# 64x64 products in the inverse of the first layer, and scores of the second layer from two-part splits with two heads in the halves of TensorE's rows

## The chip, the cores and the metric

One core of a Trainium2 chip runs the whole program. The metric is the device time of one execution in microseconds (us), as the median of several executions of the same kernel. TensorE multiplies (PE in the profile, its weight loads PEld), VectorE is DVE, ScalarE is ACT, GpSimd is POOL, and SyncE (SP) issues most DMAs.

## What is computed

Eight batches of 512 tokens with 256 features pass four stages, each added to its input: an attention layer with landmarks, a feed-forward layer with experts, a causal attention layer with rotary embedding, and the feed-forward layer again. The change touches the first and the third.

```python
# first layer: 16 heads, for each (batch, head) a 64x64 matrix attn2
z = swapaxes(a, -1, -2) / (max(col) * max(row))
for _ in range(6):
    az = a @ z
    z = 0.25 * z @ (13 * I - az @ (15 * I - az @ (7 * I - az)))
out = attn1 @ z @ (attn3 @ v)
# second attention layer: 16 heads of 16 features, T = 512
scores = einsum('bhqd,bhkd->bhqk', rotary(q), rotary(k)) * 16 ** -0.5
attn = softmax(where(causal, -inf, scores))
out = einsum('bhqk,bhkd->bhqd', attn, v) @ Wo.T
```

## The kernel before

Each layer is a block in which every engine has its own program, written in the order in which it runs; PSUM banks are handed over by semaphores (class `Fills`: a consumer waits for `full`, TensorE waits for `free`). TensorE's order is the order of the code.

**First layer (`layer_a`).** It runs batch by batch, about 110 us each. The heads stand in eight pairs, one head in partitions 0 to 63 and one in 64 to 127. The inverse of a batch is a chain of steps (`INVERSE_STEPS`), and each step is placed by `mark` between products of other work, so that VectorE and ScalarE have time to answer. Most products of the chain (line 960) are made of two 64x64 ones, in opposite quarters of the array. In the step "wz" TensorE multiplies with `p_diag`, the block-diagonal form of the polynomial: in four of the six iterations one 128x128 product per pair gives both W and Z (line 992). In the third iteration (`RESTORE`, k = 2) each pair takes two 64x64 products (line 988) and then one with all 128x128 weights and 64 columns (line 990), and in the last iteration the latter alone. A product of plain fp32 is two instructions in the trace.

**Second attention layer (`layer_b`).** The 16 heads of a batch are 8 pairs, 64 pairs in all. Queries and keys are projected (line 2644), rotated by VectorE and POOL, and split into three bf16 parts whose sum is the fp32 number (`high` and `middle` on ScalarE, `split_rest` on POOL). The parts go through DRAM (`spread` on SP) into `stacked`: six groups of 16 rows, so that one product over 96 rows sums the six products of parts that matter. Four such buffers are in use.

The program goes in slots, one per pair. In slot n the turned scores (keys in the rows, kind "st") of pair n and the plain scores (kind "s") of pair n + 7 are made, so that the row maxima are known seven slots before they are needed: VectorE takes them from the plain scores (`maximum`, lines 2379 and 2383), POOL splits them into three parts, TensorE turns them (line 2653), and they come back through DRAM as three more rows of the turned product (99 rows). ScalarE takes the exponentials of the turned scores (line 2506).

The causal scores of a pair are five units of 512 columns, `UNITS`: two of one product (line 2606 writes the mask, line 2616 the scores), two of two products (384 and 128 columns, mask by line 2610), and one with both heads in it (256 columns each, line 2602). The mask is a bf16 product of an identity with a triangle, and the scores are added to it in the bank. In each slot TensorE takes, for u = 0 to 4, unit u turned and then unit u plain; behind u = 1 the early side work (`misc_early`: transposes of x, projections, turning of the maxima), behind u = 2 the products with v (`products`, line 2674, in 128x32 tiles), behind u = 3 the late side work (`misc_late`: transposes and output projection). "st" has three banks, "s" two, the products with v one and the side work two.

## Time and profile before

| | us |
|---|---|
| median of 3 runs | 2464.02 |
| lowest, highest | 2453.02, 2469.33 |
| the profiled execution, its whole time | 2465.51 |
| span of its trace, first to last instruction | 2463.4 |
| TensorE busy in the span | 2220.4 |
| mean granted TensorE clock | 0.945 of full speed |

The first layer runs from the start to 1000 us with its landmarks, the second attention layer from about 1470 to 2015, and the feed-forward layers between and behind. Durations of products in the trace hold their way through the array, and products overlap: how fast they go is read from the distance of their starts.

### The profile page before, as it was taken

The numbers are of one execution on the slowest core, as the hardware profiler recorded it, in microseconds if no ns is written. First come the engines' busy times: TensorE is split into PE (matmuls) and PEld (weight loads), VectorE is DVE, ScalarE is ACT, GpSimd is POOL, SyncE is SP. The second block draws the span as 40 slices with busy tenths as digits, with TensorE's granted clock in tenths as the row PEclk, the third lists the DMA queues.
The fourth block names the chain that finished last, engine by engine and source line by source line (L and its number), as shares of the span: only waits on it lengthen the run. The fifth ranks groups of instructions, "written<-read, shape, count | busy, mean of one in ns | idle before, by whom it ended". The sixth has DMA issues, their size and how long they took to land. (4 is left out here: it accounts for less than half of the span.)

```text
span 2463.4 us, 49191 instructions
## 1 busy us (share of the span) xinstructions
PE 2220.4 (90%) x19494; PEld 1810.1 (73%) x19494; DVE 1457.2 (59%) x3308; ACT 1030.9 (42%) x1986; POOL 680.1 (28%) x772
## 2 busy tenths in 40 slices
PE   7799999999999999699879974899999979986998
PEld 7688888888888888577669972455555547776998
DVE  2565564647465554388746644666666627874665
ACT  4333334333333334244335531455555544432554
POOL 3210110101010100165522222433343215652222
PEclk8899999999999999799989986899999999998999
DMA  7300000000000000411547756444444416113775
GB/s 233 117 18 10 10 10 10 10 10 19 2 18 10 10 1 2 130 44 61 206 157 220 235 147 140 79 79 79 80 86 80 74 55 223 48 43 95 233 231 137
DMA packets 155901, 212.68 MB, mean 86 GB/s; under 512 B 51656, under 2 KB 140000, under 8 KB 150368
## 3 DMA queue, kind: packets, MB, share of 16 engines
q1 hardware_dynamic: 142140, 191.38, 27.6%
q0 software_dynamic: 12864, 17.38, 4.3%
q8 instruction: 158, 2.59, 0.4%
q10 hardware_dynamic: 672, 0.79, 0.2%
q14 instruction: 67, 0.55, 0.1%
HBM read 141.80 MB, written 67.69 MB: 85 GB/s over the span
## 5 line engine op out<-in xcount | busy, mean ns | idle before, releaser
L2383 DVE TENSOR_REDUCE b_neg_max<-bank 128x1 f32<-128x512 f32 (+2 forms) x384 | 179.0, 507 | 140.4 <-PE bank L2616 137.9
L2506 ACT ACTIVATE b_probsT<-bank 128x512 f32<-128x512 f32 x320 | 183.1, 603 | 180.2 <-PE bank L2616 155.0
L2113 PE MATMUL bank<-e_hT_hi,k_rwkv 128*128 128x256 f32 x1088 | 214.8, 283 | 2.8 <-DVE e_hT_lo L2016 2.8
L2113 PEld LDWEIGHTS bank<-e_hT_hi,k_rwkv 128*128 128x128 f32 x1088 | 177.0, 191 | 3.6 <-DVE e_hT_lo L2016 3.6
L789 POOL TENSOR_TENSOR probs<-probs,rcp 128x512 f32<-128x512 f32 x64 | 66.9, 1045 | 381.7 <-DVE rcp L658 381.7
L2127 PE MATMUL bank<-v_rwkv_hi,e_hidden_hi 128*128 (+1 forms) x544 | 153.5, 282 | 0.0
L2127 PE MATMUL bank<-v_rwkv_hi,e_hidden_lo 128*128 (+1 forms) x544 | 153.5, 282 | 0.0
L2113 PE MATMUL bank<-e_hT_lo,k_rwkv 128*128 128x256 f32 x544 | 152.3, 280 | 0.0
L2127 PE MATMUL bank<-v_rwkv_lo,e_hidden_hi 128*128 (+1 forms) x544 | 152.1, 280 | 0.0
L2074 ACT ACTIVATE e_relu<-bank,k_bias 128x256 f32<-128x256 f32 x272 | 113.6, 469 | 73.2 <-PE bank L2113 63.1
L2616 PE MATMUL bank<-b_k_stacked,b_q_stacked 96*128 96x512 bf16 (+3 forms) x512 | 126.5, 309 | 0.0
L2616 PE MATMUL bank<-b_q_stacked,b_k_stacked 99*128 99x512 bf16 (+3 forms) x512 | 121.7, 300 | 0.0
L960 PEld LDWEIGHTS bank<-pi_t,wz 64*64 64x64 f32 x3072 | 97.2, 134 | 32.7 <-issue 23.1
L960 PE MATMUL bank<-pi_t,wz 64*64 64x64 f32 x3072 | 110.4, 221 | 3.5 <-DVE pi_t L700 3.5
L640 DVE TENSOR_TENSOR conv_lo<-bank,conv_hi 128x512 fp32r<-128x512 f32 x64 | 44.3, 692 | 109.8 <-ACT conv_hi L805 109.8
L2035 DVE TENSOR_TENSOR e_square<-e_relu 128x512 f32<-128x512 f32 x136 | 93.9, 690 | 23.9 <-ACT e_relu L2074 16.7
L2113 PEld LDWEIGHTS bank<-e_hT_lo,k_rwkv 128*128 128x128 f32 x544 | 103.8, 191 | 0.0
L2037 DVE TENSOR_TENSOR e_hidden_lo<-e_square,e_hidden_hi 128x512 fp32r<-128x512 f32 x136 | 94.2, 692 | 14.8 <-DVE e_square L2035 0.5
L2606 PE MATMUL bank<-masks,ident 128*128 128x128 bf16 x256 | 57.5, 225 | 50.2 <-DMA b_k_stacked<-scratch_b_parts 34.2
L2127 PEld LDWEIGHTS bank<-v_rwkv_hi,e_hidden_lo 128*128 128x128 f32 x544 | 102.4, 188 | 0.0
L2127 PEld LDWEIGHTS bank<-v_rwkv_lo,e_hidden_hi 128*128 128x128 f32 x544 | 102.4, 188 | 0.0
L2127 PEld LDWEIGHTS bank<-v_rwkv_hi,e_hidden_hi 128*128 128x128 f32 x544 | 102.2, 188 | 0.0
(364 smaller groups left out, 6252.4 us busy)
## 6 DMA issues: line engine op xcount, KB each, us to landing
k_rwkv<-scratch_k SPq DMA_DIRECT2D x32, 2048.0 KB, 7.3
scratch_b_parts<-b_part SPq DMA_DIRECT2D x96, 128.0 KB, 2.1
b_q_stacked<-scratch_b_parts SPq DMA_DIRECT2D x96, 128.0 KB, 4.4
b_k_stacked<-scratch_b_parts SPq DMA_DIRECT2D x96, 128.0 KB, 4.6
e_rows<-scratch_rows SPq DMA_DIRECT2D x34, 258.0 KB, 7.7
scratch_rows<-f_hq SPq DMA_DIRECT2D x16, 516.0 KB, 8.1
x_tokens<-in_x_dram SPq DMA_DIRECT2D x8, 512.0 KB, 8.0
scratch_x_out<-x_tokens SPq DMA_DIRECT2D x8, 512.0 KB, 2.9
```

The source lines that it names most:

```text
L640: nc.vector.tensor_tensor(lo, fills.data(*name)[:], hi.bitcast(F32), ALU.subtract).then_inc(fills.released(*name), 1)
L789: nc.gpsimd.tensor_tensor(probs, probs, spread(rcp1[:, f], NP), ALU.mult).then_inc(s["probs1_done"], 1)
L960: last = nc.tensor.matmul(data[h, j * M:(j + 1) * M], lhs[h, j], rhs[h, j], start=True, stop=True)
L2035: nc.vector.tensor_tensor(flat(sq[:, q % 2]), flat(r[:, q % 2]), flat(r[:, q % 2]), ALU.mult).then_inc(s["square_done"], 1)
L2037: nc.vector.tensor_tensor(flat(h2[1][:, q % SQ_RING]), flat(sq[:, q % 2]), flat(h2[0][:, q % SQ_RING]).bitcast(F32), ALU.subtract).then_in ...
L2074: nc.scalar.activation(r[:, q % 2, n], fl.data("h", q)[:, n * ROWS:(n + 1) * ROWS], ACT.Relu, bias=ff.k_bias[i % 2][:, 2 * c + n:2 * c + n ...
L2113: last = nc.tensor.matmul(data[:, half * ROWS:(half + 1) * ROWS], ff.k_part(i % 2, a)[:, k, at:at + P], hT[b][:, i % 2, k], start=n == 0, ...
L2127: last = nc.tensor.matmul(fl.data("e", i)[:, t * C:(t + 1) * C], h2[a][:, q % SQ_RING, half, t * P:(t + 1) * P], values[b], start=chunk == ...
L2383: last = nc.vector.tensor_reduce(neg_max[:, half % 2, t, head + e:head + e + 1], data[:, at:at + (t + 1) * P], AX_X, ALU.max, negate=True)
L2506: nc.scalar.activation(probsT[:, ring, u], fl.data("st", pair, u)[:], ACT.Exp, scale=DB ** -0.5).then_inc(fl.released("st", pair, u), 1)
L2606: nc.tensor.matmul(data[:, at:at + P], ident16[:], mask[:, 0:P], start=True, stop=False, skip_group_check=True)
L2616: last = nc.tensor.matmul(data[:, at:at + size], weights[:, tile:tile + P], moving[:, first:first + size], start=False, stop=True, skip_gr ...
```

## The change

In the inverse the product of line 990 is made of two 64x64 ones, one for each head of the pair, as line 988 is. Line 992 stays as it is.

In the second attention layer:

- Queries, keys and maxima are split into two fp32r parts instead of three bf16 ones. ScalarE's `middle` and one subtraction on POOL are gone (and on VectorE for the first keys); the split of the maxima takes two steps instead of five. Three groups of 16 rows, and two of maxima, are 48 or 50 rows, and two heads stand in rows 0 to 63 and 64 to 127.
- A score product uses 64 rows of the array. In slots that have both kinds, `scores_beside` issues a product of the turned unit and one of the plain unit by turns, always with the heads in opposite halves and in two banks. Units are taken in the order 0, 1, both heads, 2, 3 (turned) and 2, 3, both heads, 0, 1 (plain).
- The mask takes two products per unit and head, since an identity of 64 rows covers half of the mask's rows.
- In the unit of both heads the halves would write one bank, so TensorE waits (`wait_for_heads`) for the first head's products to end before it issues the second's. It stands behind u = 1 and its side work instead of last.
- The maxima are turned by fp32 products. The stores are two per step instead of three, the loads still twelve per half of a batch, in rows of 2 KB instead of 1 KB; loads of maxima are two instead of one.

```diff
                                         nc.tensor.matmul(pairs[h, j, 0], wz[h, g, j, 1, :], p_diag[h, g, j, h], start=True, stop=True)
                                 if k in (RESTORE, ITERS - 1):
-                                    last = nc.tensor.matmul(pairs[:, j, 1], p_diag[:, g, j], wz[:, g, j, 1, :], start=True, stop=True)
+                                    for h in halves:
+                                        last = nc.tensor.matmul(pairs[h, j, 1], p_diag[h, g, j, h], wz[h, g, j, 1, :], start=True, stop=True)
                                 else:
                                     last = nc.tensor.matmul(pairs[:, j], p_diag[:, g, j], wz[:, g, j], start=True, stop=True)
...
-Q_PARTS, K_PARTS_B = (0, 0, 1, 1, 0, 2), (0, 1, 0, 1, 2, 0)
+Q_PARTS, K_PARTS_B = (0, 0, 1), (0, 1, 0)
+PARTS_B = 2
 STACK = len(Q_PARTS) * DB
-MAX_PARTS = 3
+MAX_PARTS = 2
+ROW_HALF = P // 2
+STACK_DMAS = 2 * 2 * len(Q_PARTS)
...
+BOTH = len(UNITS) - 1
+TURNED_ORDER, SCORED_ORDER = (0, 1, BOTH, 2, 3), (2, 3, BOTH, 0, 1)
...
-        ident16, masks = buf("ident16", [P, P], BF16), buf("masks16", [P, 2, 2 * P], BF16)
+        ident16, masks = buf("ident16", [P, 2, P], BF16), buf("masks16", [P, 2, 2, P], BF16)
...
-        parts = [buf(f"b_part{c}", [P, 2, T], BF16) for c in range(3)]
-        stacked = [[buf(f"b_{side}_stacked{b}", [P, HEADS_H, T], BF16) for b in range(STACK_BUFS)] for side in ("q", "k")]
-        neg_max, rest = buf("b_neg_max", [P, 2, TT, HEADS_H]), buf("b_max_rest", [P, TT, HEADS_H])
-        max_parts, max_rows = buf("b_max_parts", [P, 2, TT, MAX_PARTS, HEADS_H], BF16), buf("b_max_rows", [P, 2, T], BF16)
-        one_rows = buf("b_one_rows", [P, T], BF16)
+        parts = [buf(f"b_part{c}", [P, 2, T], F32R) for c in range(PARTS_B)]
+        stacked = [[buf(f"b_{side}_stacked{b}", [P, PAIRS_H, T], F32R) for b in range(STACK_BUFS)] for side in ("q", "k")]
+        neg_max = buf("b_neg_max", [P, 2, TT, HEADS_H])
+        max_parts, max_rows = buf("b_max_parts", [P, 2, TT, MAX_PARTS, HEADS_H], F32R), buf("b_max_rows", [P, 2, T])
         v = buf("b_v", [P, 2, TT, HB, 2 * DB])
         probsT = buf("b_probsT", [P, PROBS_RING, len(UNITS), T])
-        oT = buf("b_oT", [P, T])
+        one_rows = oT = buf("b_oT", [P, T])
...
-        scratch = lambda name, shape: nc.dram_tensor(f"scratch_{name}", shape, BF16, kind="Internal").ap()
-        parts_out, max_out = scratch("b_parts", (B * 4, 3, P, T)), scratch("b_max", (B * 2 + 1, MAX_PARTS * HEADS_H, T))
+        scratch = lambda name, shape: nc.dram_tensor(f"scratch_{name}", shape, F32, kind="Internal").ap()
+        parts_out, max_out = scratch("b_parts", (B * 4, PARTS_B, P, T)), scratch("b_max", (B * 2 + 1, MAX_PARTS * HEADS_H, T))
...
+                def stack(side, b, at):
+                    for row, c in enumerate((Q_PARTS, K_PARTS_B)[side]):
+                        for e in range(2):
+                            first = e * ROW_HALF + row * DB
+                            sp.dma_start(stacked[side][b][first:first + DB, :, :].bitcast(F32),
+                                         parts_out[at, c].rearrange("(j e d) t -> e d j t", e=2, d=DB)[e]).then_inc(stack_loaded[b], 16)
...
-                    g.tensor_tensor(rotated[:, at % 2], rotated[:, at % 2], parts[0][:, at % 2], ALU.subtract).then_inc(s["rest_done"], 1)
-                    ready((s["mid_done"], at + 1))
-                    g.tensor_tensor(parts[2][:, at % 2], rotated[:, at % 2], parts[1][:, at % 2], ALU.subtract).then_inc(s["lo_done"], 1)
+                    g.tensor_tensor(parts[1][:, at % 2], rotated[:, at % 2], parts[0][:, at % 2].bitcast(F32), ALU.subtract).then_inc(
+                        s["lo_done"], 1)
...
-                            exponentials(slot, u)
+                            exponentials(slot, TURNED_ORDER[u])
...
+                def mask(data, pair, u, turned, e, roll, start):
+                    rows = half_rows(e)
+                    region, src = data[:].rearrange("p (n k) -> p n k", k=P), masks[rows, int(turned), roll, :]
+                    if u == BOTH:
+                        region = region[:, 2 * e + (0 if turned else 1), :]
+                    elif len(UNITS[u]) == 1:
+                        region = region[:, 0 if turned else 3, :]
+                    else:
+                        region = region[:, 0:2, :] if turned else region[:, 0:4:3, :]
+                        src = src.unsqueeze(1).to_broadcast([ROW_HALF, 2, P])
+                    nc.tensor.matmul(region, ident16[rows, roll, :], src, start=start, stop=False, skip_group_check=True)
+                def part(data, pair, u, turned, e, n):
+                    b, j = half_of(pair) % STACK_BUFS, pair % PAIRS_H
+                    rows = half_rows(e, STACK + MAX_PARTS if turned else STACK)
+                    q, k = stacked[0][b][rows, j], stacked[1][b][rows, j]
+                    t, at = UNITS[u][e if u == BOTH else n][1:]
+                    size = (t + 1) * P
+                    tile, first = ((TT - 1 - t) * P, (TT - 1 - t) * P) if turned else (t * P, 0)
+                    weights, moving = (k, q) if turned else (q, k)
+                    return nc.tensor.matmul(data[:, at:at + size], weights[:, tile:tile + P], moving[:, first:first + size], start=False,
+                                            stop=True, skip_group_check=True)
+                def alone(one, start):
+                    for roll in range(2):
+                        mask(*one, roll, start and roll == 0)
+                    for n in range(parts_in(one[2])):
+                        last = part(*one, n)
+                    return last
+                def beside(one, other, start):
+                    for roll in range(2):
+                        mask(*one, roll, start and roll == 0)
+                        mask(*other, roll, start and roll == 0)
+                    for n in range(parts_in(one[2])):
+                        last = part(*one, n), part(*other, n)
+                    return last
+                heads_done = 0
+                def wait_for_heads(*last):
+                    nonlocal heads_done
+                    for instruction in last:
+                        instruction.then_inc(s["head_done"], 1)
+                        heads_done += 1
+                    pe.wait_ge(s["head_done"], heads_done)
                 def scores(pair, u, turned):
                     name = ("st" if turned else "s", pair, u)
-                    b, head = half_of(pair) % STACK_BUFS, pair % PAIRS_H * 2
-                    rows = slice(0, STACK + MAX_PARTS) if turned else slice(0, STACK)
-                    data = begin(*name)
-                    mask = masks[:, int(turned)]
-                    if u == last_unit:
-                        at = 0 if turned else P
-                        region = data[:].rearrange("p (h n) -> p h n", h=2)[:, :, at:at + P]
-                        nc.tensor.matmul(region, ident16[:], mask.rearrange("p (h n) -> p h n", h=2), start=True, stop=False,
-                                         skip_group_check=True)
-                    elif len(UNITS[u]) == 1:
-                        at = 0 if turned else 3 * P
-                        nc.tensor.matmul(data[:, at:at + P], ident16[:], mask[:, 0:P], start=True, stop=False, skip_group_check=True)
+                    one = (begin(*name), pair, u, turned)
+                    if u == BOTH:
+                        wait_for_heads(alone((*one, 0), True))
+                        last = alone((*one, 1), False)
                     else:
-                        region = data[:, 0:2 * P] if turned else data[:].rearrange("p (h n) -> p h n", h=4)[:, 0:4:3, :]
-                        src = mask if turned else mask.rearrange("p (h n) -> p h n", h=2)
-                        nc.tensor.matmul(region, ident16[:], src, start=True, stop=False, skip_group_check=True)
-                    for e, t, at in UNITS[u]:
-                        size = (t + 1) * P
-                        q, k = stacked[0][b][rows, head + e], stacked[1][b][rows, head + e]
-                        tile, first = ((TT - 1 - t) * P, (TT - 1 - t) * P) if turned else (t * P, 0)
-                        weights, moving = (k, q) if turned else (q, k)
-                        last = nc.tensor.matmul(data[:, at:at + size], weights[:, tile:tile + P], moving[:, first:first + size], start=False,
-                                                stop=True, skip_group_check=True)
+                        last = alone((*one, UNITS[u][0][0]), True)
                     last.then_inc(fl.filled(*name), 1)
+                def scores_beside(pair, u, ahead, w):
+                    one, other = (begin("st", pair, u), pair, u, True), (begin("s", ahead, w), ahead, w, False)
+                    if u == BOTH:
+                        wait_for_heads(*beside((*one, 0), (*other, 1), True))
+                        last = beside((*one, 1), (*other, 0), False)
+                    else:
+                        last = beside((*one, UNITS[u][0][0]), (*other, UNITS[w][0][0]), True)
+                    last[0].then_inc(fl.filled("st", pair, u), 1)
+                    last[1].then_inc(fl.filled("s", ahead, w), 1)
...
-                                                    max_parts[:, (n * 2 + name[2]) % 2, t].rearrange("p c h -> p (c h)"), ident16[:], start=True,
-                                                    stop=True)
+                            last = nc.tensor.matmul(data[ROWS, t * P:(t + 1) * P],
+                                                    max_parts[:, (n * 2 + name[2]) % 2, t].rearrange("p c h -> p (c h)").bitcast(F32),
+                                                    core.ident[:], start=True, stop=True)
...
+                        if turned_at(slot) is not None and pair is not None:
+                            scores_beside(slot, TURNED_ORDER[u], pair, SCORED_ORDER[u])
+                        elif pair is not None:
+                            scores(pair, SCORED_ORDER[u], False)
+                        elif turned_at(slot) is not None:
+                            scores(slot, TURNED_ORDER[u], True)
```

TensorE's order, in the third iteration of the inverse (the `wz` step of one group of pairs). Before:

```order
L988 MATMUL bank<-pi_p_diag,wz 64x64 x2
L990 MATMUL bank<-wz,pi_p_diag 128x64
L988 MATMUL bank<-pi_p_diag,wz 64x64 x2
L990 MATMUL bank<-wz,pi_p_diag 128x64
L988 MATMUL bank<-pi_p_diag,wz 64x64 x2
L990 MATMUL bank<-wz,pi_p_diag 128x64
```

The same place on TensorE now:

```order
L988 MATMUL bank<-pi_p_diag,wz 64x64 x2
L991 MATMUL bank<-wz,pi_p_diag 64x64 x2
L988 MATMUL bank<-pi_p_diag,wz 64x64 x2
L991 MATMUL bank<-wz,pi_p_diag 64x64 x2
L988 MATMUL bank<-pi_p_diag,wz 64x64 x2
L991 MATMUL bank<-wz,pi_p_diag 64x64 x2
```

Every product with 128x64 shape has become two of 64x64, and nothing else has moved there.

TensorE's order in one slot of the second attention layer, from a unit of two parts on (`masks` is the mask product, `b_q_stacked` as the moving side the turned scores, `b_k_stacked` the plain ones). Before:

```order
L2610 MATMUL bank<-masks,ident 128x2x128
L2616 MATMUL bank<-b_k_stacked,b_q_stacked 128x384
L2616 MATMUL bank<-b_k_stacked,b_q_stacked 128x128
L2602 MATMUL bank<-masks,ident 128x2x128
L2616 MATMUL bank<-b_q_stacked,b_k_stacked 128x256 x2
L2602 MATMUL bank<-masks,ident 128x2x128
L2616 MATMUL bank<-b_k_stacked,b_q_stacked 128x256 x2
L2606 MATMUL bank<-masks,ident 128x128
L2616 MATMUL bank<-b_q_stacked,b_k_stacked 128x512
L2606 MATMUL bank<-masks,ident 128x128
L2616 MATMUL bank<-b_k_stacked,b_q_stacked 128x512
```

The same place on TensorE now, from a unit of two parts to the next unit:

```order
L2608 MATMUL bank<-masks,ident 128x256
L2608 MATMUL bank<-masks,ident 128x2x128
L2608 MATMUL bank<-masks,ident 128x256
L2608 MATMUL bank<-masks,ident 128x2x128
L2618 MATMUL bank<-b_q_stacked,b_k_stacked 128x384
L2618 MATMUL bank<-b_k_stacked,b_q_stacked 128x384
L2618 MATMUL bank<-b_q_stacked,b_k_stacked 128x128
L2618 MATMUL bank<-b_k_stacked,b_q_stacked 128x128
L2608 MATMUL bank<-masks,ident 128x128 x4
L2618 MATMUL bank<-b_q_stacked,b_k_stacked 128x512
L2618 MATMUL bank<-b_k_stacked,b_q_stacked 128x512
```

The turned and the plain unit are no longer one behind the other but alternate product by product, with two mask products for each, and the unit of both heads has left this place.

## Rows read from the trace of the kernel before

**Rows 1.** The page, busy time of each engine over the span (us, share, instructions):

```profile
PE 2220.4 (90%) x19494; PEld 1810.1 (73%) x19494; DVE 1457.2 (59%) x3308; ACT 1030.9 (42%) x1986; POOL 680.1 (28%) x772
```

**Rows 2.** Windows of 20 us: us, busy PE, PEld, DVE, ACT, POOL, granted clock, DMA:

```profile
256.00:276.00 20.00, 20.00 (x180) 15.65 (x180) 11.56 (x23) 7.35 (x18) 3.13 (x3) 0.83 0.08 27
...
921.00:941.00 20.00, 20.00 (x228) 15.84 (x227) 13.38 (x28) 8.68 (x20) 4.25 (x5) 1.00 0.01 2
```

**Rows 3.** Timeline of TensorE in the third iteration: start, us, line, operation, count:

```profile
369.24 0.39 PE L904 MATMUL bank<-u_lo,a_xnT_hi 128*128 128x512 f32 x1
369.47 0.39 PE L904 MATMUL bank<-u_hi,a_xnT_lo 128*128 128x512 f32 x1
369.84 0.33 PE L988 MATMUL bank<-pi_p_diag,wz 64*64 64x64 f32 x4
370.10 0.43 PE L990 MATMUL bank<-wz,pi_p_diag 128*128 128x64 f32 x2
370.47 0.33 PE L988 MATMUL bank<-pi_p_diag,wz 64*64 64x64 f32 x4
...
378.68 0.63 PE L927 MATMUL bank<-a_xnT_hi,g_lo 128*128 128x512 f32 x1
```

**Rows 4.** Timeline of TensorE, other steps of the first layer:

```profile
334.64 1.95 PE L1023 MATMUL bank<-kl_diag,wqT 128*128 128x128 f32 x16
336.52 1.15 PE L960 MATMUL bank<-pi_t,wz 64*64 64x64 f32 x32
...
415.69 2.00 PE L990 MATMUL bank<-wz,pi_p_diag 128*128 128x64 f32 x16
```

**Rows 5.** Windows of the second layer, columns as in rows 2:

```profile
1600.00:1656.00 56.00, 51.09 (x401) 29.42 (x400) 35.33 (x82) 29.94 (x58) 21.43 (x23) 1.00 0.52 87
...
1936.00:2006.00 70.00, 65.47 (x576) 38.25 (x575) 29.37 (x64) 44.37 (x85) 5.52 (x13) 1.00 0.20 34
```

**Rows 6.** Timeline of TensorE in one slot of the second layer:

```profile
1702.24 0.27 PE L2602 MATMUL bank<-masks,ident 128*128 128x256 bf16 x1
...
1702.91 0.22 PE L2606 MATMUL bank<-masks,ident 128*128 128x128 bf16 x1
1702.96 0.38 PE L2616 MATMUL bank<-b_q_stacked,b_k_stacked 99*128 99x512 bf16 x1
1703.18 0.22 PE L2606 MATMUL bank<-masks,ident 128*128 128x128 bf16 x1
...
1703.46 0.27 PE L2610 MATMUL bank<-masks,ident 128*128 128x256 bf16 x1
...
1703.97 0.38 PE L2616 MATMUL bank<-b_k_stacked,b_q_stacked 96*128 96x384 bf16 x2
...
1707.06 0.38 PE L2616 MATMUL bank<-b_k_stacked,b_q_stacked 96*128 96x512 bf16 x1
1707.37 0.86 PE L2674 MATMUL bank<-b_probsT,b_v 128*32 128x256 f32 x16
```

**Rows 7.** Timeline of VectorE, the maxima of three units:

```profile
1526.93 1.35 DVE L2383 TENSOR_REDUCE b_neg_max<-bank 128x1 f32<-128x512 f32 x3 [2.84 <-PE bank L2616]
1528.22 0.69 DVE L2379 TENSOR_REDUCE b_neg_max<-bank 128x2 f32<-128x512 f32 x1
```

**Rows 8.** Lines 2616 and 1084: durations ns min/median/max, first and last start us:

```profile
L2616 PEld LDWEIGHTS bank<-b_q_stacked,b_k_stacked x512: 97/98/151, 1557.4 to 2005.2; 99*128 99x128 bf16 x171
L2616 PE MATMUL bank<-b_q_stacked,b_k_stacked x512: 217/320/634, 1557.5 to 2005.4; 99*128 99x512 bf16 x44, 99*128 99x256 bf16 x43, 99*128 99x384 bf16 x42, 99*128 99x128 bf16 x42
...
L1084 PEld LDWEIGHTS bank<-g_hi,conv_lo x256: 187/188/193, 202.7 to 995.3; 128*128 128x128 f32 x128
```

**Rows 9.** Line 2653 as in rows 8, and POOL's timeline of the first split:

```profile
L2653 PE MATMUL bank<-ident,b_max_parts x64: 219/219/314, 1548.9 to 1980.9; 128*24 128x128 bf16 x64
...
1493.60 1.15 POOL L2458 TENSOR_TENSOR b_part<-b_rotated,b_part 128x512 bf16<-128x512 f32 x1 [0.74 <-ACT b_part L2521]
```

**Rows 10.** Waits of TensorE, 1513 to 2006 us: total, times, longest:

```profile
PE bank L2606 <- DMA b_k_stacked<-scratch_b_parts: 34.2, 9, 23.3
```

110 lines of the change are left out of this document (49 added, 61 removed).

## Prediction

> **What bounds the kernel now.** I read the page first, for the shares of the engines and TensorE's clock, then tables of windows for the two places that the diff touches, then TensorE's timeline inside them, then the waits. The page says that TensorE is busy for 90% of the span [rows 1], so the question in each place is whether TensorE is what the stage waits for.
>
> In the first layer it is: in 20 us around one step of the inverse TensorE is busy for all 20, while VectorE is idle for 7 to 8 of them [rows 2]. The step meant is the third iteration's (k = 2, RESTORE), where line 988 (64x64) and line 990 (128x128 weights) alternate. The timeline shows three things. Ordinary products of 512 columns start every 0.23 us at the high clock (369.24, 369.47) [rows 3]. The alternating step has one round, four short and two long instructions, in 0.63 us (369.84 to 370.47) [rows 3], and it holds eight rounds in each of the eight batches. And the clock falls in it: at 378.68 a product of the same kind takes 0.63 us instead of 0.39 [rows 3], and the window has a mean granted clock of 0.83 against 1.00 in a batch where it does not fall [rows 2]. Of eight such windows three have 0.83, two 0.91 and three 1.00. So this is a step in which TensorE mostly empties and refills, long enough to bring its own clock down from 2.4 to 1.2 GHz.
>
> In the second layer TensorE is busy for 51.1 of 56 us, VectorE for 35.3 [rows 5]. The timeline of one slot [rows 6] gives the price of each pair of score units (turned and not): unit of two heads 0.67 us (1702.24 to 1702.91), unit of one part 0.55 (to 1703.46), unit of two parts 0.66 by its columns. Five of them, 2 x 0.55 + 2 x 0.66 + 0.67, are 3.1 us per slot. VectorE's maxima need nearly as much: three reductions of 1.35 us in a row for a one-part and a two-part unit, and 0.69 for a unit of two heads [rows 7], so about 0.61 and 0.68 per unit at pace, 3.2 us per slot. A slot takes 7.0 us (64 of them from 1557.5 to 2005.4) [rows 8]. Scores have only two banks, so TensorE can be two units ahead of VectorE and no more.
>
> **The inverse.** (a) In RESTORE the two long instructions of a round become four 64x64 ones. 64x64 products run at 32 in 1.15 us, of which the last one's own 0.22 is its way through the array: 0.030 us each [rows 4]. A round of eight is 0.24 us, 0.39 less; 64 rounds: 24.7 us. (b) In the last iteration 16 long instructions take 2.00 us [rows 4], 0.115 each, 1.84 in all; 32 short ones 0.96. Eight times 0.88 is 7 us. (c) The step becomes 1.9 us instead of 5, and no longer holds a stretch of emptying long enough for the clock to fall, as far as these rows tell. The fall cost (1 - clock) x 20 us per window: 3 x 3.4 + 2 x 1.8 = 13.8 us. Together 46 us. Nothing hides TensorE's time here, but a gain in it meets the next wait, and a tenth may be lost so: I take 42. Bounds: 32 (the clock falls elsewhere instead) and 46. The other four iterations keep their 128x128 products.
>
> **The scores, TensorE's side.** Each head gets 64 rows of the array, and the turned unit of one head runs beside the other unit of the other head. No row of before shows two products in row halves. The nearest are the 64x64 ones in opposite quarters: 0.030 us each, where one alone streams 64 columns twice, 0.053 us at 2.4 GHz [rows 4]. So I take them as overlapping; the other end (one after the other) is a rival below. The operands are now fp32r: 512 columns in 0.23 instead of 0.22 us [rows 3, 6], and 128 columns of weights load in 188 ns instead of 98 [rows 8], which shows only where a load stands behind a short product. One-part pair: masks 0.055, then the second masks and the load behind them 0.11, then 0.235: 0.40. Two-part: 0.11 + 0.11 + 0.175 + 0.06 = 0.455. The unit of two heads has both heads in one bank and now waits for the first to end: 0.055 + 0.11 + 0.28 (to the end of the product) + some 0.08 for the semaphore and the next load, then 0.055 + 0.11 + 0.12: 0.82. A slot: 0.80 + 0.91 + 0.82 = 2.53 instead of 3.1.
>
> **The same, with VectorE.** I follow the three units that stand together between the late and the early side work. Before, 1702.24 to the end of the columns of 1703.97, 0.22 later: 1.95 us [rows 6]. After: the first pair (two-part) ends at 0.455; its maximum starts 0.20 later and gives the bank back at 1.46; the second pair uses the other bank, 0.455 to 0.855; the third needs the first bank and runs from 1.46 to 1.91. So 1.93 against 1.95: nothing gained, VectorE sets it. The pair behind the early side work was 0.55 and is now the unit of two heads, 0.82 (+0.27); the one behind the products with v was 0.66 and is now 0.40 (-0.26). The scores gain nothing, 57 slots x 0. Bounds: no wait for VectorE at all, 57 x -0.56 = -32 us; no overlap, +76.
>
> The Trainium skill, in "TensorEngine Tiling (Array Packing)", PSUM Bottleneck, warns that tiling speeds up TensorE but not the emptying of PSUM, so that the copy out can become the bound. By that rule the score stage gains nothing, and by TensorE's columns alone it would gain 32 us; the walk above, made from rows, comes out on the rule's side.
>
> (d) New changes of the array's shape. Before, scores and side work (projections, transposes) were all 128x128; now every block of side work stands between 64-row scores. A change costs 0.09 us between scores and products with v (1707.06 to 1707.37 is 0.31, the columns 0.22) [rows 6], and 0.14 in RESTORE (0.63 less 4 x 0.030 and 2 x 0.115, two changes) [rows 3, 4]. Per batch of eight slots there are 13 blocks of side work; 12 new changes in at 0.14 (an fp32 load is exposed) and 11 out at 0.09 are 2.7 us; over 57 slots, 7.1 batches, +20 us. The same page (Key Properties) says that a change of tiling mode drains the engine; what it costs is only in the rows.
>
> (e) The turning of the maxima: 4 bf16 products per half, 64 in all [rows 9], at 0.055 us become fp32 ones of two instructions at 0.11 (16 in 1.95 us) [rows 4]: 0.88 - 0.22 = 0.67, 16 times: +11. (f) The split is shorter: the middle part's copy on ScalarE and one POOL subtraction of 1.15 us are gone, with the wait of 0.74 us between [rows 9], one of three stores too, and rows in DRAM are 2 KB instead of 1. TensorE's waits for the stacked keys, 34.2 us in 9 with 23.3 in the first [rows 10], leave 10.9; I take 7 of them off. (g) Start: the first chain is about 3 us shorter, but until the clock is up the masks twice over and the fp32 loads make TensorE, not VectorE, late: 0. (h) The last seven slots have turned units alone, where halves run one at a time: 2.5 instead of 1.55 us per slot, TensorE is busy for 65.5 of 70 us there [rows 5]: +7 by sum, +5 as some is covered by the exponentials. (i) ScalarE issues one DMA more per half; the maxima have spare slots, 0.
>
> Sum: 0 + 20 + 11 - 7 + 0 + 5 = +29 for the second layer, -42 for the first. The profiled execution took 2465.5 us (span 2463.4 and 2.1 around it), 1.5 above the median. 2465.5 - 42 + 29 = 2452.5, less 1.5: **2451**.
>
> **Rivals.**
> - *The score stage pays* (0.27). Side work stands in 13 of 16 gaps and lets VectorE catch up; if the waits are shorter than in my walk, up to the 32 us come off: 2420. For it: VectorE is at 63% only. Against: rows 7.
> - *Row halves do not overlap* (0.12), the one that ends slower. Place: every pair of score products. One-part 2 x 0.345 = 0.69, two-part 2 x 0.455 = 0.91, two heads 1.3. The three units take 2.5 instead of 1.95, the other two 2.0 instead of 1.2: +1.34 us, 57 times, +76: 2527. It decides once a pair takes over 1.4 times one half, since the other terms leave 13 us of gain. Against it: 64x64 pairs overlap.
> - *The clock falls in the second layer* (0.08). More emptying, as in RESTORE. A fifth of its 490 us at 1.2 GHz costs half of that, 49 us: 2500. For it: RESTORE itself; against: TensorE still streams well over half of a slot.
> - *The inverse's gain is caught by other engines* (0.05): 30 us less, 2481.
> - My forecast 0.48, of which 0.08 ends below 2439.
>
> A measurement of this kernel tells about 1% from no change. Faster by over 1% (below 2439): 0.27 + 0.08 = 0.35. Slower (above 2489): 0.12 + 0.04 = 0.16. Same: 0.49. Range for 8 in 10: from the first rival's side, 2413, to the clock's, 2494; the second rival stays out.
>
> **What would show it.** RESTORE rounds of 0.24 us and windows at clock 1.00: (a) to (c) right. Partners of a score pair starting within some 10 ns: overlap; 0.2 us apart: rival two. Three units in 1.9 us with TensorE waiting for the maxima: right; in 1.3: rival one. Gaps near 0.1 us at each block of side work: (d). Wrong if the first layer's batch of 110 us loses less than 4 us, or a slot of 7.0 us becomes over 8.

## The result: 0.8% slower, where 0.1% faster was forecast

The changed kernel takes 2476.33 us, median of 20 runs (2469.51 to 2485.99), the kernel before 2454.53 in 20 runs beside them (2446.63 to 2469.33). The ratio is 1.0079, 95% interval [1.0062, 1.0096]. The time lies in the range (2413 to 2494), but the interval is on the other side of 1 than the forecast of 2451. That forecast is 0.1% below this median of before, and it was 13 us (0.5%) below the 2464.02 known then. Its sum was -42 in the first layer and +29 in the second; apart, the two halves of the change turned out as -36 and +57.

The profiled execution of the changed kernel took 2470.23 us (span 2468.1); that of before took 2465.5, which is 11 us above the median of its 20 runs. So the stages are compared between two executions, and the totals between medians. These are the marks of both, in us from the span's start, each the start of the first or last product of its kind in the trace:

| stage | before | after | change |
|---|---|---|---|
| end of the first layer | 995.4 | 953.2 | -42.2 |
| feed-forward, to the second layer's first statistics | 478.5 | 477.7 | -0.8 |
| first statistics to first plain score | 39.4 | 36.6 | -2.8 |
| first plain to first turned score | 44.2 | 56.8 | +12.6 |
| first turned to last plain score | 419.7 | 452.6 | +32.9 |
| last plain to last turned score | 28.2 | 34.8 | +6.6 |
| the rest (output, feed-forward) | 458.0 | 456.4 | -1.6 |

The page of after, in the form of [rows 1]:

```profile
PE 2196.9 (89%) x20710; PEld 1788.1 (72%) x20710; DVE 1457.5 (59%) x3307; ACT 1019.5 (41%) x1955; POOL 637.2 (26%) x693
```

TensorE is busy for 24 us less than before and the time is longer: 1216 instructions more, and more standing between them.

**First layer.** Windows of 20 us around the third iteration in after, as [rows 2], and its timeline, as [rows 3]:

```profile
245.00:265.00 20.00, 20.00 (x255) 16.07 (x254) 17.24 (x36) 8.97 (x22) 4.18 (x4) 1.00 0.09 29
...
560.00:580.00 20.00, 20.00 (x263) 15.94 (x263) 16.70 (x34) 8.15 (x20) 4.18 (x4) 1.00 0.09 28
```

```profile
252.01 0.33 PE L988 MATMUL bank<-pi_p_diag,wz 64*64 64x64 f32 x4
252.17 0.28 PE L991 MATMUL bank<-wz,pi_p_diag 64*64 64x64 f32 x4
252.29 0.28 PE L988 MATMUL bank<-pi_p_diag,wz 64*64 64x64 f32 x4
252.41 0.28 PE L991 MATMUL bank<-wz,pi_p_diag 64*64 64x64 f32 x4
252.52 0.28 PE L988 MATMUL bank<-pi_p_diag,wz 64*64 64x64 f32 x4
```

A round of eight runs from 252.29 to 252.52, 0.23 to 0.24 us, as forecast. The granted clock is 1.00 without a break from 108 to 958 us, so in all eight batches, and VectorE works 16 to 17 of the 20 us instead of 11 to 14.

**Second layer.** Windows of the steady part, as [rows 5]:

```profile
1557.00:1613.00 56.00, 48.53 (x486) 27.13 (x488) 36.54 (x87) 27.97 (x53) 17.33 (x18) 1.00 0.45 93
...
1837.00:1893.00 56.00, 50.02 (x434) 29.19 (x430) 31.97 (x75) 25.28 (x49) 13.88 (x16) 0.92 0.36 72
```

TensorE is busy for 48.5 of 56 us, where it was 51.1: it waits more. The stretch from the first plain to the first turned score, in before and then in after:

```profile
1513.30:1557.50 44.20, 34.09 (x132) 17.24 (x133) 28.49 (x62) 8.45 (x15) 16.72 (x18) 0.73 0.51 90
```

```profile
1467.50:1524.30 56.80, 45.40 (x190) 26.10 (x188) 28.81 (x62) 6.27 (x11) 11.82 (x11) 0.65 0.46 96
```

Here TensorE has more to do, and at a lower clock: 39.8 us of the stretch are at 1.2 GHz, 23.7 before. Its waits in the steady part, from 1550 to 1940, beside [rows 10]:

```profile
PE bank L2608 <- DVE b_neg_max L2395: 38.6, 61, 1.0
PE bank L2688 <- DVE b_xn L2360: 3.4, 6, 0.6
```

No wait for the stacked keys is left in that stretch, and one kind has come in their place: for a bank that VectorE's maxima still read. The timeline of TensorE in one slot shows it (an extract; 48 and 50 rows are the plain and the turned side of a pair):

```profile
1742.84 0.39 PE L2608 MATMUL bank<-masks,ident 64*128 64x256 bf16 x4
1742.99 0.42 PE L2618 MATMUL bank<-b_q_stacked,b_k_stacked 50*128 50x384 f32 x1
1742.99 0.42 PE L2618 MATMUL bank<-b_k_stacked,b_q_stacked 48*128 48x384 f32 x1
...
1743.32 0.29 PE L2608 MATMUL bank<-masks,ident 64*128 64x128 bf16 x4
...
1744.44 0.39 PE L2608 MATMUL bank<-masks,ident 64*128 64x256 bf16 x4 [0.55 <-DVE b_neg_max L2395]
...
1744.86 0.22 PE L2618 MATMUL bank<-b_k_stacked,b_q_stacked 48*128 48x128 f32 x1
...
1747.17 0.28 PE L2608 MATMUL bank<-masks,ident 64*128 64x128 bf16 x4
...
1747.72 0.29 PE L2608 MATMUL bank<-masks,ident 64*128 64x128 bf16 x4
...
1748.11 1.71 PE L2722 MATMUL bank<-b_probsT,b_v 128*32 128x512 f32 x16
```

Partners start within some 10 ns of each other (1742.99 twice), so the halves of the rows do run at once. The two-part pair takes 0.48 us (1742.84 to 1743.32). Then the third pair stands until 1744.44, 1.60 after the first began, and the three take 2.08 us with the last one's 0.48. The unit of both heads takes 0.94 (1747.17 to 1748.11), half after half.

This is the wait where three pairs stand together behind late side work. Where a slot has no late side work, four pairs follow each other behind the products with v, and it is longer. VectorE and then TensorE there (an extract; the first pair began at 1725.32):

```profile
1725.88 0.73 DVE L2371 STREAM_SHUFFLE b_swapped<-bank 128x512 f32<-128x512 f32 x1
1726.50 2.72 DVE L2395 TENSOR_REDUCE b_neg_max<-bank 128x1 f32<-128x512 f32 x5
```

```profile
1727.33 0.29 PE L2608 MATMUL bank<-masks,ident 64*128 64x128 bf16 x4 [0.97 <-DVE b_neg_max L2395]
```

VectorE has the rotation of the queries or keys to do before the maxima, so the third pair starts 2.01 us after the first.

### The profile page after: what moved, and what is told of

It is laid out like the page before. It is cut to its first block and busy times, and to the rows that moved or that the text cites. A ratio compares the mean times of both kernels' runs of the same rounds, so it can differ in the third digit from the quotient of the medians.

```text
span 2468.1 us, 51756 instructions
## 1 busy us (share of the span) xinstructions
PE 2196.9 (89%) x20710; PEld 1788.1 (72%) x20710; DVE 1457.5 (59%) x3307; ACT 1019.5 (41%) x1955; POOL 637.2 (26%) x693
## 5 line engine op out<-in xcount | busy, mean ns | idle before, releaser
L2608 PE MATMUL bank<-masks,ident 64*128 64x128 bf16 (+1 forms) x1536 | 138.6, 244 | 85.0 <-DVE b_neg_max L2395 50.6
L2608 PEld LDWEIGHTS bank<-masks,ident 64*128 64x128 bf16 x1536 | 50.6, 95 | 200.8 <-issue 138.3
L2618 PE MATMUL bank<-b_k_stacked,b_q_stacked 48*128 48x512 f32 (+3 forms) x512 | 171.4, 387 | 0.0
L2618 PE MATMUL bank<-b_q_stacked,b_k_stacked 50*128 50x512 f32 (+3 forms) x512 | 165.7, 374 | 0.0
L2461 POOL TENSOR_TENSOR b_swapped<-b_swapped,sin 128x512 f32<-128x512 f32 x31 | 39.5, 1275 | 320.6 <-DVE b_swapped L2371 320.6
L2391 DVE TENSOR_REDUCE b_neg_max<-bank 128x2 f32<-128x512 f32 x64 | 44.3, 692 | 113.0 <-PE bank L2618 113.0
L640 DVE TENSOR_TENSOR conv_lo<-bank,conv_hi 128x512 fp32r<-128x512 f32 x64 | 44.3, 692 | 109.8 <-ACT conv_hi L805 109.8
```

Source lines behind the costliest of these rows:

```text
L640: nc.vector.tensor_tensor(lo, fills.data(*name)[:], hi.bitcast(F32), ALU.subtract).then_inc(fills.released(*name), 1)
L2608: nc.tensor.matmul(region, ident16[rows, roll, :], src, start=start, stop=False, skip_group_check=True)
L2618: return nc.tensor.matmul(data[:, at:at + size], weights[:, tile:tile + P], moving[:, first:first + size], start=False, stop=True, skip_gr ...
```

## The experiments

Twelve kernels, all timed beside runs of before: four together (before 2455.35), four later (2455.92), four later again (2455.29). The standing of each is its ratio to before. Differences between kernels of different sets are given as differences of medians; by the ratios they come out up to 3 us different. "Time at the low clock" is that of the falls that begin in the stretch.

### The halves of the change apart

e1_inverse is the kernel before with the inverse's edit alone, e2_scores the changed kernel without it:

```
-  last = nc.tensor.matmul(pairs[:, j, 1], p_diag[:, g, j], wz[:, g, j, 1, :], ...)
+  for h in halves:
+      last = nc.tensor.matmul(pairs[h, j, 1], p_diag[h, g, j, h], wz[h, g, j, 1, :], ...)
```

> The kernel before with the inverse's edit alone. Theory A (the two parts add up, and the first layer's 42 us of the two traces are real in the medians too): 32 to 42 us faster than before, ratio 0.983 to 0.987; the end of the first layer comes at about 953 us as in the changed kernel, the second attention layer stays as before. Rival B (part of the 42 us was only the clock falling in the one profiled execution of before, while the median of before falls less): 20 to 30 us, ratio 0.988 to 0.992. In both, the RESTORE step takes about 2 us instead of 5.

> The changed kernel with the inverse as before, so the scores alone. Theory A: the scores lose what the whole change and the inverse differ by, 22 + 32 to 42 = 54 to 64 us, ratio 1.022 to 1.026. Rival B: 42 to 52 us, ratio 1.017 to 1.021. My recorded sum was +29 us (1.012); if that comes, both are wrong and the parts disturb each other.

Measured: e1_inverse 2419.57 us, ratio 0.9859 [0.983, 0.9888]; e2_scores 2511.92, ratio 1.0236 [1.0204, 1.0268]. So -35.8 and +56.6, together +20.8 against +21.8 for both: Theory A in both, the halves of the change add, and nothing of the inverse's gain was caught. In the profiled execution e1_inverse ends its first layer at 952.9 and e2_scores at 993.4. The first layer of before has 27.2 us at the low clock from falls that begin between 100 us and its end, that of e2_scores 20.4, and those of after and of e1_inverse none.

### The bank that the maxima hold

```
-  homes = {"st": (0, 1, 2), "s": (3, 4), ...
+  homes = {"st": (0, 1), "s": (2, 3, 4), ...
```

> The changed kernel with three PSUM banks for the plain scores and two for the turned ones, instead of two and three. Theory C (TensorE waits 0.55 us per slot, and up to 1 in some, because the plain scores may be only two units ahead of VectorE's maxima): 15 to 30 us faster than the changed kernel, the waits of TensorE for b_neg_max, 38.6 us in 61 between 1550 and 1940, go to below 15. Rival D (VectorE or ScalarE is behind anyway, so that a bank only moves the wait to the turned side): within 5 us, and the waits for b_probsT rise by as much.

Measured: 2452.93, ratio 0.9995 [0.9974, 1.0016], so 23 us less than the changed kernel (Theory C). The first turned to the last plain score takes 428.6 instead of 452.6. TensorE's waits in it, 1550 to 1900:

```profile
PE bank L2608 <- ACT b_probsT L2514: 19.2, 46, 1.6
PE bank L2688 <- DVE b_xn L2360: 4.6, 6, 1.0
```

The wait for VectorE is gone and a shorter one for ScalarE's exponentials has come, since turned units now have two banks. At the end, where only turned units are made, that costs: 43.2 us from the last plain to the last turned score, 34.8 in after.

Where the 24 us come from is told by the traces. TensorE's records of the steady part are summed here by kind of place, each from its first start to the start of the next kind of work, in us, waits included (two incomplete places at the ends are left out):

| place, and how many | before | after | e3 |
|---|---|---|---|
| three pairs between late and early side work, 27 | 72.5 | 63.9 | 61.8 |
| four pairs, where there is no late side work, 16 | 49.6 | 50.2 | 41.9 |
| four or five pairs, where there is no early side work, 13 | 47.2 | 53.9 | 41.6 |
| the pair behind early side work, 44 | 28.4 | 41.7 | 41.3 |
| the pair behind the products with v, 39 | 26.2 | 21.5 | 20.2 |
| side work, 85 blocks | 125.6 | 148.1 | 144.7 |
| products with v, 55 | 67.3 | 71.2 | 75.1 |

The bank gives 20.6 of its 24 us where four or five pairs stand in a row, and 2.1 in the 27 places of three that the timeline above shows: there the next wait, for the input of the side work, takes up what the bank saves.

Whether the bank would have helped before as well is asked by e10_inverse_banks, e1_inverse with the same line changed:

> e1_inverse (the scores of before, the inverse of after) with two banks for turned and three for plain units. Theory A (the third plain bank is worth 23 us only because a pair now takes a bank of each kind at once, with both maxima behind it): within 5 us of 2420. Theory B (two plain banks held before back as well): 8 to 20 us less, about 2405, and then the bank is no merit of the row halves.

Measured: 2425.33, ratio 0.9872 [0.9844, 0.99], 6 us more than e1_inverse (3 by the ratios). The intervals overlap, so it is nearest to Theory A: the third plain bank is worth nothing to single units, and much to pairs.

### The maxima, turned

e4_max_r is the changed kernel with the parts of the maxima turned as fp32r products, by a copy of the identity in fp32r:

```
-  ....rearrange("p c h -> p (c h)").bitcast(F32), core.ident[:], start=True, stop=True)
+  ....rearrange("p c h -> p (c h)"), ident_r[:], start=True, stop=True)
```

> The changed kernel, with the maxima turned by fp32r products (the parts are fp32r, the identity gets an fp32r copy) instead of plain fp32. If TensorE sets the end there, 8 instructions of 0.109 us become 4 of about 0.06 in each of 16 places: 0.63 x 16 = 10 us faster than the changed kernel. If the time is taken up by waits for VectorE behind it: under 4 us.

Measured: 2464.08, ratio 1.0035 [1.0018, 1.0053], 12 us less than the changed kernel, where 10 were expected if TensorE sets the end. Line 2701 (2702 in e4) from 1550 to 1950, in after and then in e4:

```profile
L2701 PE MATMUL bank<-ident,b_max_parts x96: 272/273/283, 1573.0 to 1927.6; 128*16 128x128 f32 x96
```

```profile
L2702 PE MATMUL bank<-ident_r,b_max_parts x48: 218/224/412, 1573.3 to 1927.2; 128*16 128x128 f32 x48
```

Twelve halves in that stretch: eight instructions of each as fp32, four as fp32r. A block of side work that is one such half alone takes 0.33 us in before, 0.98 in after and 0.35 in e4.

### The wait between the heads

e5_heads_late is the changed kernel with the products with v between the first and the second halves of the unit of both heads:

```
-  wait_for_heads(*beside((*one, 0), (*other, 1), True))
+  mark_heads(*beside((*one, 0), (*other, 1), True))
+  products(*pv_at(pair))
+  pe.wait_ge(s["head_done"], heads_done)
   last = beside((*one, 1), (*other, 0), False)
```

> The changed kernel, with the products with v issued between the first and the second halves of the unit of both heads, so that TensorE does not stand at the semaphore between the halves. Theory A (that wait is a real cost): the unit took 0.94 us with about 0.2 to 0.25 of standing in it, 57 times, so 10 to 14 us less than the changed kernel (2476), about 2463. Theory B (the time goes to VectorE's maxima and their banks, so a filled wait only moves the standing to the next bank): within 4 us of 2476, or more, since VectorE gets the maxima of both heads 1.4 us later.

Measured: 2520.04, ratio 1.0245 [1.0217, 1.0274], 44 us more. Neither theory had this size. VectorE's timeline in e5 shows where it comes from:

```profile
1750.97 1.32 DVE L2395 TENSOR_REDUCE b_neg_max<-bank 128x1 f32<-128x512 f32 x3
1754.56 0.69 DVE L2391 TENSOR_REDUCE b_neg_max<-bank 128x2 f32<-128x512 f32 x1 [2.27 <-PE bank L2618]
```

VectorE stands 2.27 us until the unit of both heads is complete, and its three next maxima come behind it. Its waits for that unit are 132.3 us in 44 (1550 to 1940), where after has 77.3 in 49. TensorE then waits in turn (at 1747.99 for 1.17 us), and the time at the low clock, 27.2 us of the steady part in after, is 81.6 in e5: of the 50 us by which the steady part is longer (502.8), half of that difference is 27, and TensorE is idle for 29 us more. So the unit ahead of the products with v is what VectorE lives on while they run. What the wait between the heads costs by itself is not shown by this run.

### Both units in the same half

e6_same_rows takes the two units of a pair from the same head, so that they need the same rows:

```
-  TURNED_ORDER, SCORED_ORDER = (0, 1, BOTH, 2, 3), (2, 3, BOTH, 0, 1)
+  TURNED_ORDER, SCORED_ORDER = (0, 1, BOTH, 2, 3), (0, 1, BOTH, 2, 3)
```

(and heads 0, 0 and 1, 1 in the unit of both.)

> The changed kernel, with the turned unit and the plain unit of a pair taken from the same head, that is in the same half of the rows, so that they cannot run at once; the instructions and their number are the same. Theory A (the halves do overlap, and TensorE sets the pace of the slot together with the banks): a one-part pair takes 0.69 instead of about 0.45, a two-part pair 0.91 instead of about 0.5, both heads 1.3 instead of 0.94, so 1.0 to 1.5 us per slot, 57 to 86 us more: 2530 to 2560. Theory B (VectorE sets the pace): less than 20 us more.

Measured: 2633.38, ratio 1.0732 [1.0703, 1.076], 157 us more, and more than either theory had. The steady part is 151 us longer (603.6 instead of 452.6, by the same marks), 191 us of it at the low clock; in after 27.2. At half speed these 164 us more are about 82 us of the 151, and the other 69 are 1.2 us a slot, inside the 1.0 to 1.5 of Theory A, which had no term for the clock. Partners start a third of a microsecond apart:

```profile
1745.49 0.48 PE L2618 MATMUL bank<-b_q_stacked,b_k_stacked 50*128 50x512 f32 x1
1745.81 0.40 PE L2618 MATMUL bank<-b_k_stacked,b_q_stacked 48*128 48x512 f32 x1
```

### Changes of the array's shape

e7_late_by_pv has fewer: the late block of side work stands behind the products with v (`if u == 3:` becomes `if u == 2:`, in the order and on TensorE). e12_more_changes is e3_s_banks with one 128x128 product more ahead of the last pair of each full slot:

```
+  if u == TURNED_ORDER[-1]:
+      nc.tensor.matmul(other[0][:, 0:P], ident16[:, 0, :], masks[:, 0, 0, :], start=True, stop=True)
   last = beside((*one, ...), (*other, ...), True)
```

> The changed kernel, with the late block of side work moved from behind the fourth pair of score units to behind the products with v, so that a slot with late side work has two changes of the array's shape fewer. Theory A (each change costs some 0.1 us that nothing hides): 6 of 8 slots, 7 batches, 2 changes of 0.1 us: 8 us less than the changed kernel, about 2468. Theory B (the late block is where VectorE catches up with TensorE, and two score units more now stand in a row): 5 to 15 us more, about 2485, with TensorE's wait for the maxima longer than 38.6 us in 1550:1940.

> e3_s_banks with one 128x128 product of 128 columns ahead of the last pair of each full slot, whose result is overwritten: two changes of the array's shape and one short product more, 57 times. Theory A (TensorE sets the pace there and each change costs 0.10 us): 57 x (0.20 + 0.06) = 15 us more than e3_s_banks (2453), about 2468. Theory B (changes lie beside waits): less than 5 us more.

Measured: e7 2481.09, ratio 1.0104 [1.0082, 1.0126], 5 us more than the changed kernel; TensorE's wait for the maxima is 33.2 us, not longer, and 34.0 us of the steady part are at the low clock (27.2). So the time is Theory B's, but not by the wait that it named.

e12 2464.23, ratio 1.0035 [1.0013, 1.0058], 11 us more than e3. The edit does less than its expectation says: in 39 of the 57 places the inserted product stands behind late side work, which is 128x128 itself, and adds no change of shape; only in the other 18 are there two more. The inserted product and what follows it:

```profile
1741.94 0.22 PE L2665 MATMUL bank<-masks,ident 128*128 128x128 bf16 x1
1742.09 0.39 PE L2608 MATMUL bank<-masks,ident 64*128 64x256 bf16 x4
```

0.15 us from start to start, where 128 columns of bf16 follow each other in 0.055 [rows 6]: 0.10 for the change back. By such distances a product costs 0.06 us in the 39 places and 0.25 in the 18, 7 us in all. The steady part is 10.5 us longer than e3's (439.1), and half of its additional time at the low clock (20.5 us for 10.2) is 5 of them. So the price of a change stands by its rows, and the 11 us are not a measure of it.

The traces of before and after show the same price without an insertion. A block of four fp32 products, and the next scores, in before and then in after:

```profile
1701.80 0.60 PE L2658 MATMUL bank<-ident,b_oT 128*128 128x128 f32 x4
1702.24 0.27 PE L2602 MATMUL bank<-masks,ident 128*128 128x256 bf16 x1
```

```profile
1702.24 0.66 PE L2706 MATMUL bank<-ident,b_oT 128*128 128x128 f32 x4
1702.83 0.39 PE L2608 MATMUL bank<-masks,ident 64*128 64x256 bf16 x4
```

0.44 and 0.59 us. Out of side work, the last fp32 product of 128 columns and the next scores start 0.109 us apart in before and 0.205 in after. Into side work, a score product of 128 columns is followed in 0.055 us before and 0.148 after, where its own columns take 0.06; behind one of 512 columns it is 0.40, where they take 0.23. For the 85 blocks of the steady part that makes some 18 us of TensorE's time (an estimate from these distances).

### The start

From the first plain to the first turned score it is 44.2 us before and 56.8 after. e8_start_pairs issues the plain units there two heads at a time, in the order (2, 0), (3, 1), both heads:

```
+  both = [(begin("s", pair, i), pair, i, False, UNITS[i][0][0]) for i in (u, w)]
+  ... beside(*both, True)
```

e11_warm issues products in TensorE's wait for the first keys:

```
+  idle = begin("s", pair, SCORED_ORDER[0])
+  for i in range(72):
+      nc.tensor.matmul(idle[:], ident16[:, 0, :], masks[:]..., start=True, stop=True)
```

> The changed kernel, with the plain units of the seven slots before the first turned unit issued two heads at a time (the units of one head beside those of the other), not one half of the rows at a time. The stretch from the first plain score to the first turned one grew from 44.2 to 56.8 us by the change. Theory A (it grew because units alone leave half of the array idle): 5 to 9 us come back, about 2469. Theory B (it grew because of the low clock and the longer blocks of side work there): less than 3 us, within the measurement of 2476.

> The changed kernel with 72 products of 512 columns whose result is not used, issued in TensorE's wait of some 20 us for the first stacked keys. Nothing is waited for by them. Theory A (the stretch from the first plain to the first turned score, 56.8 instead of 44.2 us, grew because the denser instructions run at 1.2 GHz there): it becomes 5 to 10 us shorter, about 2468. Theory B (the clock falls again after a few microseconds in that stretch whatever ran ahead of it): less than 3 us.

Measured: e8 2476.07, ratio 1.0082 [1.006, 1.0105]; e11 2478.36, ratio 1.009 [1.0062, 1.0119]. Nothing gained by either; the stretch is 60.1 us in e8 and 55.4 in e11. In e8 a pair needs both plain banks free before it begins: TensorE waits 19.3 us for the maxima in that stretch (11.4 and 7.9), where after waits 8.5 (4.7 and 3.8). In e11 the idle products do hold the clock up while they run, and it falls as before behind them. Windows of e11, then of after (from 27 us before the first plain score):

```profile
1445.00:1472.00 27.00, 22.36 (x84) 9.57 (x84) 11.13 (x23) 1.89 (x3) 9.20 (x8) 0.94 0.78 174
1472.00:1500.00 28.00, 22.85 (x96) 14.50 (x97) 13.44 (x30) 3.14 (x7) 3.80 (x3) 0.68 0.50 99
```

```profile
1440.00:1467.00 27.00, 8.35 (x12) 3.29 (x12) 10.96 (x23) 2.21 (x4) 8.79 (x8) 0.63 0.73 176
1467.00:1495.00 28.00, 23.00 (x96) 14.66 (x97) 13.46 (x30) 3.14 (x7) 3.80 (x3) 0.68 0.48 99
```

### What is left when both costs are taken away

e9_all_fixes is the changed kernel with e4's edit and

```
+  homes = {"st": (0, 1) if scored(name[1]) is not None else (0, 1, 2, 3, 4),
+           "s": (2, 3, 4) if name[1] >= LEAD else (0, 1, 2, 3, 4), "pv": (5,), "misc": (6, 7)}[kind]
```

> The changed kernel (inverse and scores) with the maxima turned as fp32r, and the banks dealt by phase: two for turned and three for plain units while both are made, all five for the one kind that is made before and after. Theory A (the two costs are separate, and the tail of e3_s_banks, 43.2 us instead of 34.8, was its missing bank): 2476 less 23 for the banks, 12 for the maxima and some 8 for the tail: 2433, so faster than before by 0.9% but slower than e1_inverse (2420). Theory B (both remove the same waits): 2445 to 2452.

Measured: 2442.7, ratio 0.9945 [0.9924, 0.9966]: 34 us less than the changed kernel, 13 less than before, between the two theories. The start is 50.3 us (56.8), the steady part 432.5 (452.6), the end 32.5 (34.8). It is the best kernel with row halves, and e1_inverse, which leaves the scores alone, is 23 us better still. In e9's steady part TensorE still stands for ScalarE (1550 to 1900), which e1_inverse does for 1.4 us:

```profile
PE bank L2610 <- ACT b_probsT L2516: 21.9, 46, 2.7
```

## Why the prediction was wrong, step by step

**The inverse: right.** (a) A round takes 0.235 us, forecast 0.24. (b) The 32 short instructions of the last iteration start within 0.9 us (292.0 to 292.9), forecast 0.96. (c) The clock does not fall in any batch. The stage went down by 42.2 us against 42 forecast, with 27.2 us of low clock gone from it; by medians the edit is worth 36 (e1). The profiled execution of before was one of the longer ones: I took it as 1.5 us above the median of the 3 runs then shown, and 20 runs put it 11 above. Against the true median the same sum, -13, is 2441.5 and not 2451, so the miss is 35 us and not 25: 28 of it in the second layer (57 for 29) and 6 in the first (36 for 42).

**Where the second layer's 28 us are.** The start and the steady part of the traces, split into three: TensorE idle between two products; half of all time at the low clock, also of falls that began before the stretch; and the rest, which is TensorE's own work at full clock. It is an estimate, since idle time at the low clock is counted in both.

| us | before | after | e3 |
|---|---|---|---|
| start, idle | 10.1 | 11.4 | 8.3 |
| start, half of the low clock | 11.8 | 19.9 | 19.0 |
| start, the rest | 22.2 | 25.6 | 24.4 |
| steady part, idle | 31.3 | 58.9 | 44.3 |
| steady part, half of the low clock | 5.3 | 15.7 | 6.7 |
| steady part, the rest | 383.1 | 378.0 | 377.6 |

In the steady part the forecast's terms were: TensorE's own work -32 by the columns, +20 for (d) and some +10 of (e), so -2, and it is -5; waits +32, by which VectorE takes back the columns' gain, less 7 of (f), so +25, and they are +28; the clock 0, and it is +10. The trace of e1_inverse, whose scores are those of before, has 27.9, 2.8 and 383.4: against it the waits are +31 and the clock +13.

**The steps that failed: the clock at nothing in the sum, and (g), "0" for the start.** The clock was only a rival, with 0.08 and 49 us. It is 10 us of the steady part and 8 of the 12.6 us of the start, where 39.8 us instead of 23.7 are at 1.2 GHz; so about 18 of the 28 us (23 against the trace of e1_inverse). The reason given for (g) was that TensorE would be late there and not VectorE; that is so (TensorE's own work is 3.4 us more), but nothing was put down for it. More banks take 5.2 us (e3), the fp32r turning 3.2 (e4) and both 6.5 (e9) off the start; idle products ahead (e11) and pairs of heads (e8) do not shorten it by more than 1.4. Why the clock falls more often is open: no run holds it still, and in e3, with one bank more, the steady part loses 9 us less to it and waits 15 us less. So the 24 us of the bank can't be parted from the clock by these runs.

**"The scores gain nothing, 57 slots x 0": about right, in part by luck.** The mechanism was right: halves overlap, VectorE's maxima set the pace, and the gain of TensorE's columns does not come. The places of score pairs sum to +7 us, 3.7 of it the clock. But the walk took one place for all. It had the third pair start 1.46 us after the first, and it was 1.60; it had pairs of 0.455, and they take 0.48: 2.08 instead of 1.93 (1.91 by its own steps). Yet the 27 places of that kind are 8.6 us shorter than before. In the place of before that the walk read [rows 6], TensorE waits too, behind the last pair, for the input of the side work, and the walk stopped ahead of that:

```profile
1705.49 1.40 PE L2640 MATMUL bank<-ident,b_xn 128*128 128x128 f32 x8 [1.13 <-DVE b_xn L2346]
```

The 29 places with four or five pairs in a row, which the walk left out, are 7.3 us longer, and a third bank for plain units takes 20.6 us off them (e3). The unit of both heads was put at 0.82 and takes 0.94, 13.3 us more in its 44 places, forecast 12. As I read it, a pair holds a bank of each kind until both are written, and the next pair needs the later of two; with units issued singly (e10) the third plain bank is worth nothing.

**(e), the maxima turned: right,** 11 forecast, 12 measured. **(f), the shorter split: right in kind,** the waits for stacked keys are gone from the steady part and the first chain is 2.8 us shorter. **(h), the end: right,** +6.6 for +5.

**(d), changes of shape: right as TensorE's time.** 0.10 us out of side work and 0.09 to 0.17 into it, where 0.09 and 0.14 were taken: some 18 us for 20 (19 by its own figures). What they cost in the end stays open: e7 took some away for nothing, and where a wait for VectorE follows, a change can lie beside it.

## What to carry to other kernels

When an edit makes a producer work in pairs, count the buffers by the pair: the next pair needs the later of two consumers, and one buffer more for the slower consumer may decide the sign, as here from 0.8% slower to level. A walk through one place has to be made for every order that the slots have: the place walked here became shorter than before, and the places with more pairs in a row, which were left out, became longer. Where the prediction itself finds that the clock fell once for work of the same kind, the clock belongs into the sum and not only among the rivals. And the two halves of a change should be timed apart first: here one was worth 36 us, and it was hidden under the 57 of the other.

## What the chip showed that was not expected

- Delaying one unit behind 0.8 to 1.7 us of other products cost 44 us in 57 slots (e5), though TensorE had nothing more to do; by the trace some 27 of them are the low clock.
- Between 128x128 side work and products of 64 rows each way costs 0.09 to 0.17 us: 0.205 us from start to start instead of 0.109 out of it, 0.148 instead of 0.055 into it.
- Two row halves of 50 and 48 rows, each with 512 columns of fp32r, ran at once with no loss to be seen: the records last 0.47 us, as one alone does (0.48 in e6).
- The time at the low clock in the steady part was 0 us in e1_inverse, 27.2 in after, 81.6 in e5 and 191 in e6. From 1524 to 1944 TensorE was busy for 393 of 420 us in e6, at a mean clock of 0.86, and for 377 in e3, at 0.98: the one that was busier had the lower clock.
- 72 idle products kept the clock at 0.94 ahead of the start, and it was at 0.68 over the next 28 us, as without them.
